# Second layer: reload of the split rows paced by units, the batch two ahead prepared four units sooner, the root ahead of the gathers, and a later store of the row numbers

## The chip, the cores and the metric

One core of one Trainium2 chip runs the whole kernel in one launch. The metric is the device time in microseconds (us), as the median of several runs. Engines are named as the profile names them: PE is TensorE's matmul, PEld its weight load, DVE is VectorE, ACT is ScalarE, POOL is GpSimd, SP is SyncE. SPq marks DMAs that SP's queue issues.

## The reference

Two layers over `x` of 16 batches x 512 rows x 128 columns. The first adds a linear attention (with rotary embedding) and a mixture of experts; the second adds a chunked softmax attention and a gated MLP with a one-row shift. Cut to what matters:

```python
x = L0_attn_x                                   # (16, 512, 128)
xn = layernorm(x)
probs = softmax(xn @ router_w.T)                # 8 experts
topk_p, topk_i = top_k(probs, 2)                # two experts for each row, weights normed to 1
x = x + linear_attention(xn) @ Wo.T + shared_mlp(xn) + sum_e(combine[:, e] * mlp_e(xn))

xn = layernorm(x)
q, k, v = split(xn @ W_qkv.T)                   # 16 heads of 8
for ci in range(n_chunks):                      # chunks of 64 rows, keys up to the chunk's end
    probs = softmax(q_c @ k_c.T / sqrt(8))
    stim = probs.sum(-1)                        # through two steps of a small recurrence
    gate = sigmoid(fhn_dynamics(stim, a, b, dt).mean(-1))
    probs = probs * (0.5 + 0.5 * gate); probs = probs / (probs.sum(-1) + 1e-8)
    out_c = probs @ v_c
x = x + out @ W_out.T + sigmoid(xr @ W_r.T) * (square(relu(xk @ W_k.T)) @ W_v.T)
```

## The kernel before

Each engine runs its own program, written out by hand; semaphores tie them together. Three stages follow one another.

**Stage one** is the first layer's attention and router, batch by batch. It scatters each row's normed copy into a table in HBM, `xs_d`, sorted by expert.

**Stage two** is the experts: 72 tiles of 256 rows (`tile` on every engine). For a tile SP reads the tile's first row and expert out of a table and issues three loads, the rows (`load_rows`, L454) and two weights (`load_weights`, L461 and L462), up to three tiles ahead. PE turns the rows (L1877), multiplies by the first weights (L1889) and by the second (L1898, for the tile before); ACT takes the relu, DVE squares it and copies the result out (L1435, L1441). In tiles 0 to 15 DVE also plans (`planning`): which tiles belong to which expert, and at last, in tile 14, which row of the experts' output belongs to each row of the batches. That last step (L1303) raises `rows_ready`. SP stores these numbers to HBM (`idx_d`, L516) in its step for tile 15, ahead of tile 15's weights and tile 16's rows; they are first loaded back after tile 32.

**Stage three** is the second layer, 17 turns (`body2`, `over_layer2`) for 16 batches. A turn b of PE has 40 units (s, u): four sheets of four heads, ten units each. In each unit PE computes one or two blocks of scores of batch b+1, of which only the row maximum is wanted (`max_scores`, L1944, 44 in a turn; DVE reduces each by `row_max`, L1471, counted as m = 1 to 44), then a block of the shifted scores of batch b (`shifted_scores`, L1967), whose exponential ACT takes (`exp_scores`, L907), and between them products with V (`pv`, L1766). The two banks for the maxima let PE run one block ahead of DVE's reads: the block m + 2 waits for DVE's read of block m.

Round this core lie the steps for other batches, placed by hand at a unit or at an m:

- for b+2: on DVE the two expert outputs are added (`combine`, L1452, m = 2 to 5), the norm's sums taken (`ln_stats_of`, `ln_means`, m = 6 to 8), on POOL the root (`ln_root`, seven small operations, L589 to L601), on DVE the norm (`ln`, m = 14 and 15), on PE the turn (`turn_xn`, (1, 6)) and q and k (`q_rows`, (1, 8) and (1, 9)). Three bf16 parts of q and k are split off by ACT and PE (`hi2`, `mid2`, `lo2`, `take_part`, from (2, 0) to (3, 0)), stored to HBM by SP (`store_parts2`, L497), and loaded back in another layout (`load_half`, L485: two halves of eight DMAs). The first half is wanted by the first `max_scores` of the batch, the second half by its 23rd.
- for b+3: on POOL eight gathers (`gather`, L651), one for 128 rows each, read the experts' output into `hT`.
- for b-1: on POOL, DVE and ACT the recurrence `fhn_*`. It begins with `reweigh_den` on DVE (L1505, m = 16), `fhn_stimulus` on POOL (L665, L667), and `reweigh_scale` on DVE (L1510, m = 18), which waits for L667 by the semaphore `fhn_floor`. At a turn's end DVE writes `output` (L1531), and POOL stores it (L721).

POOL's order in a turn is: the gathers for b+3, the root for b+2, the recurrence for b-1, the store of b-1.

```python
            def reweigh_scale(b):

                dve.wait_ge(fhn_floor, b.at(1, 1 - L2))
                nc.vector.reciprocal(fhn[6][:, :, :], fhn[1][:, :, :]).then_inc(fhn_scale, 1)
```

Of the kernel before, what the change touches and what calls it, by code (L numbers as in the profile page):

```python
# [18 lines left out]
J = T // 128  # L19
# [87 lines left out]
def build(nc, io, out):  # L107
    ctx = ExitStack()
    with ctx:
# [261 lines left out]
        def _(sp):  # L371
# [116 lines left out]

            def store_parts2(n):
                copied = value(sp, n.own(16 * QK_LOADS, -16 * QK_LOADS * HALVES))  # L490
                split_ = [value(sp, n.at(2, c + 1 - 2 * L2)) for c in range(2)]
                for c in range(2):
                    sp.wait_ge(lo_part, split_[c])
                    for h in range(2):
                        if not n.less(L2 + 2):
                            sp.wait_ge(half_loaded[n.p][h], copied)
                    sp.dma_start(parts_d[n.p, c].rearrange("a p t -> p a t"), parts[c][:, :, :]).then_inc(parts_stored[c], 16)  # L497
# [10 lines left out]
            def tile(t):  # L508
# [5 lines left out]
                if k == STRAIGHT * TB - 1:  # L514
                    sp.wait_ge(rows_ready, 1)
                    sp.dma_start(idx_d.rearrange("b p k -> p b k"), idx_all[:, :].rearrange("p (b k) -> p b k", b=B)).then_inc(rows_stored, 16)  # L516
# [13 lines left out]
                if k == LOOPED * TB:  # L530
                    sp.wait_ge(rows_stored, 16)
                    for p in range(2):
                        sp.wait_ge(xa_stored[p], 16 * HALVES)
                    for n in (FIRST, SECOND):
                        load_route(n)
                        load_xa(n)
# [21 lines left out]
            def body2(b):  # L558
                if within(b):
                    shift_rows(b, 1)  # L560
                if within(b + 4):
                    load_route(b + 4)
                    load_xa(b + 4)
                if within(b + 2):
                    store_parts2(b + 2)
                if within(b + 1):
                    shift_rows(b + 1, 0)
                if within(b + 2):
                    load_half(b + 2, 0)
                    load_half(b + 2, 1)  # L570
# [7 lines left out]
        def _(pool):  # L578
# [168 lines left out]
            def body2(b):  # L747
                if within(b + 3):
                    gather(b + 3)
                if within(b + 2):  # L750
                    ln_root(b + 2)
# [11 lines left out]
        def _(act):  # L763
# [198 lines left out]
            def body2(b):  # L962
                core, front, after, before_ = within(b), within(b + 2), within(b + 1), within(b + -1)
                for s in range(SHEETS):
                    for u in range(UNITS):
# [9 lines left out]
                        if at == (1, 4) and after:  # L975
# [3 lines left out]
                        if at == (1, 7) and front:  # L979
                            evac_xnT(b + 2)  # L980
                        if at == (2, 1) and before_:
                            tanh_gate(b + -1)
                        if at in ((2, 0), (2, 2)) and front:
                            hi2(b + 2, u // 2)
                        if at in ((2, 4), (2, 6)) and front:
                            mid2(b + 2, u // 2 - 2)
                        if at in ((2, 8), (3, 0)) and front:
                            lo2(b + 2, s - 2)
# [15 lines left out]
        def _(dve):  # L1004
# [572 lines left out]
            def body2(b):  # L1577
# [3 lines left out]
                def between(m):  # L1581
# [10 lines left out]
                    if m in (6, 7) and front:  # L1592
                        ln_stats_of(b + 2, range(2 * (m - 6), 2 * (m - 6) + 2), False)
                    if m == 8 and front:
# [6 lines left out]
                    if m in (14, 15) and front:  # L1601
                        ln(b + 2, False, range(2 * (m - 14), 2 * (m - 14) + 2))
# [34 lines left out]
        def _(pe):  # L1637
# [416 lines left out]
            def body2(b):  # L2054
# [12 lines left out]
                for s in range(SHEETS):  # L2067
                    for u in range(UNITS):
# [18 lines left out]
                        if where == (1, 2) and after:  # L2087
                            v_rows(b + 1)
                        if where == (1, 6) and front:
                            turn_xn(b + 2, False)  # L2090
                        if where in ((1, 8), (1, 9)) and front:
                            q_rows(b + 2, u - 8)
                        if where in ((2, 2), (2, 4)) and front:
                            take_part(b + 2, u // 2 - 1, 0)
                        if where in ((2, 6), (2, 8)) and front:
                            take_part(b + 2, u // 2 - 3, 1)
# [80 lines left out]
```

## Time and profile before

| | |
|---|---|
| median of 3 runs | 1700.74 us (1698.26 to 1703.08) |
| the profiled execution's own time | 1698.97 us |
| its span, first to last instruction | 1696.8 us, mean granted TensorE clock 0.946 |
| busy share of the span | PE 87%, DVE 70%, PEld 55%, ACT 49%, POOL 31% |
| stage one / two / three | about 0 to 570 / 570 to 884 / 884 to 1697 us |

The page lists what is busy where, not what a stage is worth. The longest stage is the third, so the turn is the unit to look at: DVE's L1531 ends each one, and from one L1531 to the next is one turn. The views used below are the windows (busy time of each engine, granted clock and DMA share in a stretch) and the timelines of single engines.

### The profile page before, as it was taken

How to read it: one execution, taken by the hardware profiler on the slowest of the kernel's cores; microseconds unless marked ns; L12 is line 12 of the kernel's file. 1: busy time of each engine (PE TensorE's matmuls, PEld its weight loads, DVE VectorE, ACT ScalarE, POOL GpSimd, SP SyncE). 2: the span in 40 equal slices, each digit the busy share in tenths (PEclk: the TensorE clock that was granted, in tenths of full speed). 3: DMA queues.
4: the chain of work that ended last, by engine and by line, in shares of the span. 5: the costliest groups of instructions: out<-in, count | busy, mean ns of one | idle time of the engine just before them, and what ended most of it. 6: DMA issues, size and time to landing. Idle time of an engine off the chain costs nothing.

```text
span 1696.8 us, 35053 instructions
## 1 busy us (share of the span) xinstructions
PE 1473.1 (87%) x12952; PEld 934.1 (55%) x12952; DVE 1185.6 (70%) x2666; ACT 823.2 (49%) x1565; POOL 531.9 (31%) x967
## 2 busy tenths in 40 slices
PE   4899998999888798999987988898888898889994
PEld 2566666666666587998873443343444343444431
DVE  4888778788777494455765777777677776778751
ACT  2344344334432333344325656666556665557772
POOL 2422332332331011162314234433434423432223
PEclk7999999999998998999998999999999999999996
DMA  3111111111110656777861345433344433344400
GB/s 109 40 38 45 46 39 45 46 39 45 39 33 26 163 163 200 220 238 215 251 156 51 64 101 101 94 76 71 66 97 101 91 71 73 68 94 83 82 9 12
DMA packets 119082, 152.84 MB, mean 90 GB/s; under 512 B 31348, under 2 KB 83700, under 8 KB 114292
## 3 DMA queue, kind: packets, MB, share of 16 engines
q1 hardware_dynamic: 105992, 120.25, 29.2%
q0 software_dynamic: 12928, 30.43, 6.2%
q8 instruction: 101, 1.65, 0.4%
q14 instruction: 61, 0.50, 0.1%
HBM read 109.01 MB, written 41.09 MB: 88 GB/s over the span
## 4 chain that ended last, share of the span: by engine, by line
PE 55%; DVE 27%; issue 6%; another core or an unknown queue 5%; ACT 2%; SPq 2%; POOL 1%; DMA 1%; DVEq 0%; POOLq 0%; ACTq 0%
PE bank L1766 8%; PE bank L1944 8%; DVE nmax L1471 7%; PE bank L1898 7%; PE bank L1889 7%; PE bank L1967 6%; DVE P L1166 5%; PE bank L1723 3%; PE bank L1666 2%; PE bank L1751 2%; PE bank L1907 2%; PE bank L1783 1%; PE bank L2014 1%; PE bank L1922 1%
## 5 line engine op out<-in xcount | busy, mean ns | idle before, releaser
L1471 DVE TENSOR_REDUCE nmax<-bank 128x1 f32<-128x512 f32 (+3 forms) x704 | 433.9, 636 | 189.0 <-PE bank L1944 144.6
L907 ACT ACTIVATE P<-bank 128x512 f32<-128x512 f32 x640 | 373.8, 597 | 298.8 <-PE bank L1967 230.2
L1944 PE MATMUL bank<-KT,QT 76*128 76x512 bf16 (+3 forms) x1024 | 260.5, 314 | 76.4 <-DVE nmax L1471 48.2
L1967 PE MATMUL bank<-QT,KT 78*128 78x512 bf16 (+3 forms) x1024 | 256.5, 313 | 22.2 <-ACT P L907 13.7
L1944 PEld LDWEIGHTS bank<-KT,QT 76*128 76x128 bf16 x1024 | 88.7, 99 | 265.4 <-DVE nmax L1471 149.2
L609 POOL DMA_INDIRECT xs_d<-xn,idx x128 | 126.1, 985 | 324.0 <-DVE idx L1146 284.6
L1166 DVE TENSOR_TENSOR P<-bank,early_w 128x512 f32<-128x512 f32 x256 | 160.1, 684 | 71.6 <-remote 56.0
L1766 PE MATMUL bank<-P,V 128*32 128x512 f32 (+3 forms) x2048 | 203.4, 471 | 0.0
L871 ACT ACTIVATE hr<-bank 128x512 f32<-128x512 f32 x144 | 86.0, 597 | 192.2 <-PE bank L1889 175.1
L1967 PEld LDWEIGHTS bank<-QT,KT 78*128 78x128 bf16 x1024 | 100.1, 100 | 101.7 <-ACT P L907 39.1
L1435 DVE TENSOR_TENSOR hT<-hr 128x512 f32<-128x512 f32 x144 | 98.2, 691 | 79.1 <-ACT hr L871 77.8
L1889 PE MATMUL bank<-P 128*128 128x256 f32 x576 | 141.0, 389 | 5.0 <-issue 5.0
L1898 PEld LDWEIGHTS bank<-P,hT 128*128 128x128 f32 x1152 | 140.3, 193 | 7.2 <-issue 3.0
L1898 PE MATMUL bank<-P,hT 128*128 128x128 f32 x1152 | 141.3, 276 | 0.6 <-DVE P L1441 0.6
L639 POOL DMA_DIRECT2D ys_d<-P x72 | 52.4, 727 | 252.9 <-DVE P L1441 246.7
L1889 PEld LDWEIGHTS bank<-P 128*128 128x128 f32 x576 | 107.3, 195 | 18.9 <-issue 6.4
L651 POOL DMA_INDIRECT hT<-ys_d,idx x104 | 99.5, 957 | 41.9 <-issue 33.9
L1723 PEld LDWEIGHTS bank<-P,QT 32*128 32x128 f32 x2048 | 70.1, 193 | 59.9 <-issue 59.7
L1723 PE MATMUL bank<-P,QT 32*128 32x128 f32 x2048 | 83.6, 291 | 20.0 <-DVE P L1166 15.9
L1751 PE MATMUL bank<-P,V 128*32 128x128 f32 x2048 | 86.6, 282 | 13.7 <-issue 13.5
L808 ACT COPY oT<-bank 128x512 f32<-128x512 f32 x64 | 37.4, 584 | 97.4 <-PE bank L1751 53.3
L777 ACT ACTIVATE t<-t 128x512 f32<-128x512 f32 x32 | 20.2, 631 | 124.9 <-DVE t L1044 124.9
(233 smaller groups left out, 2263.1 us busy)
## 6 DMA issues: line engine op xcount, KB each, us to landing
P<-in_fc SPq DMA_DIRECT2D x72, 256.0 KB
P<-in_proj SPq DMA_DIRECT2D x72, 256.0 KB
QT<-parts_d SPq DMA_DIRECT2D x96, 192.0 KB
parts_d<-parts SPq DMA_DIRECT2D x32, 384.0 KB, 2.5
P<-xs_d SPq DMA_DIRECT2D x72, 128.0 KB
ys_d<-P POOLq DMA_DIRECT2D x72, 128.0 KB
KT<-parts_d SPq DMA_DIRECT2D x64, 128.0 KB
KT<-parts_d SPq DMA_DIRECT2D x32, 192.0 KB
```

The costliest lines, as they stand in the source:

```text
L609: nc.gpsimd.indirect_dma_start(xs_d[:, :], bass.IndirectOffsetOnAxis(ap=idx[n.p][:, k:k + 1], axis=0), xn[n.p][:, k % J, :], None).then_in ...
L651: nc.gpsimd.indirect_dma_start(gathered_rows(n)[:, k, :], None, rows, bass.IndirectOffsetOnAxis(ap=idx[n.p][:, k:k + 1], axis=0)).then_inc ...
L907: nc.scalar.activation(P[s % 2][:, u, :], bank[k % 2][:, :], ACT.Exp, scale=float(DH) ** -0.5).then_inc(s_sb, 1)
L1166: nc.vector.tensor_tensor(P[s % 2][:, g, :].rearrange("p (j c) -> p j c", c=128), bank[g][:, :].rearrange("p (j c) -> p j c", c=128), tri[ ...
L1471: nc.vector.tensor_reduce(nmax[:, s // TWO, h:h + TWO * nh - 1:TWO, j], max_bank(n, k)[:, 0:nh * w].rearrange("p (h w) -> p h w", h=nh), A ...
L1723: ins = pe.matmul(bank[g][:, tile], kS[b.p][quad, s, tile], qf[b.p][quad, tile], start=True, stop=True)
L1751: ins = pe.matmul(OT[32 * g:32 * g + 32, tile], values(b, j, s, g), P[s % 2][:, g, tile], start=False, stop=(s % TWO == 1 and j == J - 1), ...
L1766: ins = pe.matmul(OT[32 * g:32 * g + 32, 128 * kb:T], values(b, kb, s, g), P[s % 2][:, u, c:c + n], start=(s % TWO == 0 and k == 0), stop= ...
L1889: ins = pe.matmul(w[:, i * GT:(i + 1) * GT], wfc[t.p][:, c * 128:(c + 1) * 128], xgT[t.p % 2], start=True, stop=True)
L1898: ins = pe.matmul(bank[6][:, c * 128:(c + 1) * 128], hT[:, t.p % 2, k, c * 128:(c + 1) * 128], wpj[t.p][:, k, :], start=(k == 0), stop=(k ...
L1944: ins = pe.matmul(max_bank(n, k)[:, i * w:(i + 1) * w], QT[n.p][0:MROWS, h, j * 128:(j + 1) * 128], KT[n.p][0:MROWS, h, 0:w], start=True, ...
L1967: ins = pe.matmul(bank[k % 2][:, c:c + n], KT[b.p][0:SROWS, h, 128 * kb:128 * kb + 128], QT[b.p][0:SROWS, h, 128 * kb:T], start=True, stop ...
```

## The change

It has three parts.

1. **Row numbers.** The wait for `rows_ready` and the store of `idx_d` move from SP's step for tile 15 to its step for tile 32; the loads that read them move from tile 32 to tile 33.
2. **Reload.** SP's eight loads of a half are issued one by one, each after a wait for a unit of PE's (`load_half_at`). The first half of batch b+2 is issued between units 27 and 37 of turn b, the second half of batch b+1 between units 1 and 16 of turn b. Before, both halves were issued in a row at the end of a turn. The two shift rows and the loads for b+4 are now issued between them.
3. **Preparation of b+2.** `ln_stats_of` for all four blocks of rows at m = 6, `ln_means` at m = 7, `ln` at m = 11 and 12 (was 14 and 15); `turn_xn` at (1, 2) (was (1, 6)), `q_rows` at (1, 4) and (1, 5) (was (1, 8), (1, 9)), the splitting four units sooner; `v_rows` and `evac_v2` one and two units sooner. On POOL the root for b+2 comes ahead of the gathers for b+3.

```diff
+            def load_half_at(n, h, b, pieces):
+
+                for k, u in pieces:
+                    sp.wait_ge(s_ps, b.at(PASS, u + 1 - PASS * L2))
+                    load_half(n, h, LOADS[k:k + 1])
...
-                if k == STRAIGHT * TB - 1:
-                    sp.wait_ge(rows_ready, 1)
-                    sp.dma_start(idx_d.rearrange("b p k -> p b k"), idx_all[:, :].rearrange("p (b k) -> p b k", b=B)).then_inc(rows_stored, 16)
...
                 if k == LOOPED * TB:
+                    sp.wait_ge(rows_ready, 1)
+                    sp.dma_start(idx_d.rearrange("b p k -> p b k"), idx_all[:, :].rearrange("p (b k) -> p b k", b=B)).then_inc(rows_stored, 16)
+                if k == LOOPED * TB + 1:
                     sp.wait_ge(rows_stored, 16)
...
             def body2(b):
+                second_half = within(b + 1) and not b.less(L2 + 1)
+                if second_half:
+                    load_half_at(b + 1, 1, b, [(0, 1), (1, 3), (2, 5), (3, 7)])
                 if within(b):
                     shift_rows(b, 1)
+                if second_half:
+                    load_half_at(b + 1, 1, b, [(4, 10), (5, 12), (6, 14), (7, 16)])
                 if within(b + 4):
                     load_route(b + 4)
                     load_xa(b + 4)
                 if within(b + 2):
                     store_parts2(b + 2)
+                if within(b + 2):
+                    load_half_at(b + 2, 0, b, [(0, 27), (1, 28), (2, 29)])
                 if within(b + 1):
                     shift_rows(b + 1, 0)
                 if within(b + 2):
-                    load_half(b + 2, 0)
-                    load_half(b + 2, 1)
+                    load_half_at(b + 2, 0, b, [(3, 31), (4, 32), (5, 34), (6, 35), (7, 37)])
...
             def body2(b):
+                if within(b + 2):
+                    ln_root(b + 2)
                 if within(b + 3):
                     gather(b + 3)
-                if within(b + 2):
-                    ln_root(b + 2)
...
-                    if m in (6, 7) and front:
-                        ln_stats_of(b + 2, range(2 * (m - 6), 2 * (m - 6) + 2), False)
-                    if m == 8 and front:
+                    if m == 6 and front:
+                        ln_stats_of(b + 2, range(J), False)
+                    if m == 7 and front:
                         ln_means(b + 2)
...
-                    if m in (14, 15) and front:
-                        ln(b + 2, False, range(2 * (m - 14), 2 * (m - 14) + 2))
+                    if m in (11, 12) and front:
+                        ln(b + 2, False, range(2 * (m - 11), 2 * (m - 11) + 2))
...
-                        if where == (1, 2) and after:
+                        if where == (1, 1) and after:
                             v_rows(b + 1)
-                        if where == (1, 6) and front:
+                        if where == (1, 2) and front:
                             turn_xn(b + 2, False)
-                        if where in ((1, 8), (1, 9)) and front:
-                            q_rows(b + 2, u - 8)
+                        if where in ((1, 4), (1, 5)) and front:
+                            q_rows(b + 2, u - 4)
+                        if where in ((1, 8), (2, 0)) and front:
+                            take_part(b + 2, s - 1, 0)
                         if where in ((2, 2), (2, 4)) and front:
-                            take_part(b + 2, u // 2 - 1, 0)
-                        if where in ((2, 6), (2, 8)) and front:
-                            take_part(b + 2, u // 2 - 3, 1)
+                            take_part(b + 2, u // 2 - 1, 1)
...
```

POOL, a turn of the steady part of stage three, before: the store of a finished batch (`out`), the gathers (`hT<-ys_d`), the root (`std`, `rstd`), the first steps of the recurrence (`fhn`).

```order
L721 DMA out<-early_w 128x4x128 [waits out_ready,rows_stored]
L651 DMA hT<-ys_d,idx 128x128 [waits x1_ready,route_loaded0,rows_stored]
L651 DMA hT<-ys_d,idx 128x128 x7
L589 TENSOR_TENSOR std<-mv,lnc 128x4 [waits ln_mean]
L591 TENSOR_TENSOR rstd<-std,lnc 128x4 [waits ln_step]
L593 TENSOR_TENSOR std<-std,rstd 128x4 [waits ln_step]
L595 TENSOR_TENSOR std<-std,rstd 128x4 [waits ln_step]
L597 TENSOR_TENSOR std<-std,lnc 128x4 [waits ln_step]
L599 TENSOR_TENSOR std<-std,lnc 128x4 [waits ln_step]
L601 TENSOR_TENSOR rstd<-rstd,std 128x4 [waits ln_step]
L665 TENSOR_TENSOR fhn<-yb,rden 128x64 [waits fhn_den]
L667 TENSOR_SCALAR fhn<-fhn 128x64 [waits fhn_stim]
```

The same place of the changed kernel (its line numbers are 12 higher here):

```order
L733 DMA out<-early_w 128x4x128 [waits out_ready,rows_stored]
L601 TENSOR_TENSOR std<-mv,lnc 128x4 [waits ln_mean]
L603 TENSOR_TENSOR rstd<-std,lnc 128x4 [waits ln_step]
L605 TENSOR_TENSOR std<-std,rstd 128x4 [waits ln_step]
L607 TENSOR_TENSOR std<-std,rstd 128x4 [waits ln_step]
L609 TENSOR_TENSOR std<-std,lnc 128x4 [waits ln_step]
L611 TENSOR_TENSOR std<-std,lnc 128x4 [waits ln_step]
L613 TENSOR_TENSOR rstd<-rstd,std 128x4 [waits ln_step]
L663 DMA hT<-ys_d,idx 128x128 [waits x1_ready,route_loaded0,rows_stored]
L663 DMA hT<-ys_d,idx 128x128 x7
L677 TENSOR_TENSOR fhn<-yb,rden 128x64 [waits fhn_den]
L679 TENSOR_SCALAR fhn<-fhn 128x64 [waits fhn_stim]
```

The root and the gathers have changed places: the gathers now stand behind a wait for `ln_mean`, and directly ahead of the recurrence's first step.

SP, the same part of a turn, before: the second half of a batch's reload, the shift rows, the loads for b+4, the store of the parts.

```order
L485 DMA QT<-parts_d 24x4096 [waits parts_stored0,s_ps]
L485 DMA QT<-parts_d 24x4096 x2
L485 DMA KT<-parts_d 24x4096 [waits parts_stored1]
L485 DMA KT<-parts_d 16x4096
L485 DMA KT<-parts_d 8x4096 x2
L485 DMA KT<-parts_d 16x4096
L506 DMA QT<-shift 1x32x128 [waits shift_hi,s_ps]
L506 DMA QT<-shift 1x32x128 [waits shift_lo]
L468 DMA wts<-wts_d 128x8 [waits x1_ready]
L469 DMA idx<-idx_d 128x8
L474 DMA xt<-xa_d 128x512 [waits res_ready]
L497 DMA parts_d<-parts 128x3x512 [waits half1_loaded1,half0_loaded1,lo_part] x2
```

The same in the changed kernel (L512 is `shift_rows`, L503 `store_parts2`):

```order
L485 DMA QT<-parts_d 24x4096 [waits parts_stored0,s_ps]
L485 DMA QT<-parts_d 24x4096 [waits s_ps] x2
L485 DMA KT<-parts_d 24x4096 [waits parts_stored1,s_ps]
L512 DMA QT<-shift 1x32x128 [waits shift_hi,s_ps]
L512 DMA QT<-shift 1x32x128 [waits shift_lo]
L485 DMA KT<-parts_d 16x4096 [waits s_ps]
L485 DMA KT<-parts_d 8x4096 [waits s_ps] x2
L485 DMA KT<-parts_d 16x4096 [waits s_ps]
L468 DMA wts<-wts_d 128x8 [waits x1_ready]
L469 DMA idx<-idx_d 128x8
L474 DMA xt<-xa_d 128x512 [waits res_ready]
L503 DMA parts_d<-parts 128x3x512 [waits half1_loaded1,half0_loaded1,lo_part] x2
```

Every load of the half has a wait of its own for `s_ps`, PE's count of shifted scores, and the shift rows stand in the middle of them.

## Rows read from the trace of the kernel before

**Rows 1.** Page, busy us of each engine; windows of the three stages
```profile
PE 1473.1 (87%) x12952; PEld 934.1 (55%) x12952; DVE 1185.6 (70%) x2666; ACT 823.2 (49%) x1565; POOL 531.9 (31%) x967
...
core 0: us, PE busy (x) PEld busy (x) DVE busy (x) ACT busy (x) POOL busy (x), PEclk, DMA share, GB/s
0.00:570.00 570.00, 485.83 (x6034) 346.49 (x6034) 425.56 (x1126) 217.49 (x393) 167.74 (x255) 0.96 0.16 47
570.00:884.00 314.00, 290.82 (x1948) 265.89 (x1947) 195.59 (x378) 112.44 (x230) 84.61 (x110) 0.97 0.70 209
884.00:1697.00 813.00, 696.40 (x4973) 321.73 (x4972) 564.49 (x1163) 493.24 (x942) 279.58 (x602) 0.92 0.37 74
```

**Rows 2.** Windows of turns 5, 13 and 2 to 12, same columns
```profile
1138.22:1189.22 51.00, 44.47 (x318) 20.79 (x317) 37.33 (x79) 31.38 (x60) 19.17 (x40) 0.93 0.41 84
1547.47:1591.51 44.04, 41.46 (x318) 19.55 (x317) 37.10 (x78) 31.41 (x60) 11.83 (x32) 1.00 0.41 82
...
986.81:1547.47 560.66, 489.16 (x3478) 227.43 (x3477) 410.60 (x859) 344.71 (x660) 210.61 (x440) 0.93 0.41 84
```

**Rows 3.** Timeline of PE, turn 5: start, length, [idle before <-releaser]
```profile
1149.99 0.34 PE L1944 MATMUL bank<-KT,QT 76*128 76x384 bf16 x1 [1.51 <-issue]
...
1153.03 0.50 PE L1944 MATMUL bank<-KT,QT 76*128 76x384 bf16 x1 [2.49 <-DVE nmax L1471]
```

**Rows 4.** Timeline of POOL, turn 5
```profile
1140.69 1.04 POOL L651 DMA_INDIRECT hT<-ys_d,idx  x1 [0.30 <-issue]
...
1150.52 0.21 POOL L589 TENSOR_TENSOR std<-mv,lnc 128x4 f32<-128x4 f32 x1
...
1153.05 0.20 POOL L601 TENSOR_TENSOR rstd<-rstd,std 128x4 f32<-128x4 f32 x1
1163.77 0.35 POOL L665 TENSOR_TENSOR fhn<-yb,rden 128x64 f32<-128x64 f32 x1 [10.52 <-DVE rden L1505]
1164.20 0.40 POOL L667 TENSOR_SCALAR fhn<-fhn 128x64 f32<-128x64 f32 x1
```

**Rows 5.** Timeline of POOL, turn 0: the second burst of gathers begins
```profile
904.05 1.00 POOL L651 DMA_INDIRECT hT<-ys_d,idx  x1 [0.54 <-issue]
```

**Rows 6.** Timeline of PE, turn 0, in that burst
```profile
910.45 0.39 PE L1944 MATMUL bank<-KT,QT 76*128 76x512 bf16 x1 [0.80 <-issue]
...
916.16 0.34 PE L1944 MATMUL bank<-KT,QT 76*128 76x384 bf16 x1 [2.00 <-DVE nmax L1471]
```

**Rows 7.** Windows of turn 0, with the columns of rows 1
```profile
911.00:916.50 5.50, 2.93 (x31) 1.32 (x29) 2.38 (x4) 2.25 (x5) 2.20 (x3) 1.00 0.15 39
...
916.00:921.00 5.00, 4.84 (x14) 2.08 (x15) 2.01 (x5) 2.59 (x6) 0.00 (x0) 0.66 0.00 0
```

**Rows 8.** Timeline of SP's queue at tiles 14 and 15
```profile
623.74 0.38 SPq L462 DMA_DIRECT2D P<-in_proj  x1
637.27 0.38 SPq L516 DMA_DIRECT2D idx_d<-idx_all  x1
```

**Rows 9.** Timeline of DVE: the last step of the plan
```profile
636.96 0.29 DVE L1303 TENSOR_TENSOR idx_all<-P,moved 128x128 int32<-128x128 f32 x1
```

**Rows 10.** Timeline of PE, tiles 14 to 17
```profile
630.05 1.89 PE L1889 MATMUL bank<-P 128*128 128x256 f32 x8
...
640.91 0.69 PE L1877 MATMUL bank<-ident,P 128*128 128x128 f32 x2 [7.00 <-DMA P<-xs_d]
643.21 3.75 PE L1889 MATMUL bank<-P 128*128 128x256 f32 x8 [1.61 <-issue]
...
649.26 1.89 PE L1889 MATMUL bank<-P 128*128 128x256 f32 x8
...
652.99 1.89 PE L1889 MATMUL bank<-P 128*128 128x256 f32 x8
```

**Rows 11.** Timeline of DVE, turn 13
```profile
1547.47 0.69 DVE L1531 TENSOR_TENSOR early_w<-xr,bank 128x512 f32<-128x512 f32 x1 [0.56 <-PE bank L1994]
...
1557.04 0.37 DVE L1021 BATCH_NORM_AGGREGATE mv<-stats 128x2 f32<-128x6 f32 x4
...
1567.03 0.54 DVE L1510 RECIPROCAL fhn<-fhn 128x64 f32<-128x64 f32 x1
```

**Rows 12.** Timeline of PE, turn 13
```profile
1566.58 0.39 PE L1944 MATMUL bank<-KT,QT 76*128 76x512 bf16 x1 [0.53 <-DVE nmax L1471]
...
1568.52 0.34 PE L1944 MATMUL bank<-KT,QT 76*128 76x384 bf16 x1
...
1568.92 1.02 PE L1907 MATMUL bank<-xnT,wqkv 128*128 128x512 f32 x2
1569.78 0.33 PE L1944 MATMUL bank<-KT,QT 76*128 76x384 bf16 x1
...
1580.71 0.39 PE L1967 MATMUL bank<-QT,KT 78*128 78x512 bf16 x1 [0.57 <-ACT P L907]
```

More of the change, by code:

```diff
@@ L974, in body2 @@
                             evac_oT(b + -1, 1)
-                        if at == (1, 4) and after:
+                        if at == (1, 2) and after:
                             evac_v2(b + 1)
@@ L978, in body2 @@
                             evac_oT(b, 0)
-                        if at == (1, 7) and front:
+                        if at == (1, 3) and front:
                             evac_xnT(b + 2)
@@ L982, in body2 @@
                             tanh_gate(b + -1)
+                        if at in ((1, 6), (1, 8)) and front:
+                            hi2(b + 2, u // 2 - 3)
                         if at in ((2, 0), (2, 2)) and front:
-                            hi2(b + 2, u // 2)
+                            mid2(b + 2, u // 2)
                         if at in ((2, 4), (2, 6)) and front:
-                            mid2(b + 2, u // 2 - 2)
-                        if at in ((2, 8), (3, 0)) and front:
-                            lo2(b + 2, s - 2)
+                            lo2(b + 2, u // 2 - 2)
                         if at == (2, 8) and after:
```

## The prediction, made blind

> **What bounds the kernel.** I read the page first: PE is busy 87% of the span [rows 1], and next to it comes DVE with 70%. Then the windows of the three stages: the third is the longest, 813 us, and has the lowest granted clock, 0.92 against 0.96 and 0.97 [rows 1]. So I cut stage three into turns, from one DVE L1531 to the next, and asked the windows for two of them [rows 2]. Turn 5 takes 51.00 us, turn 13 takes 44.04. Both run 318 matmuls and the same DMA share, 0.41. They differ in one thing: POOL runs 40 operations in turn 5 and 32 in turn 13, because the last gathers belong to turn 12. The 6.96 us split cleanly. PE is busy 3.01 us longer (44.47 against 41.46) at a mean clock of 0.93 against 1.00, and idle 3.95 us longer (6.53 against 2.58). The idle time has a place: two gaps of 1.51 and 2.49 us, at 1149.99 and 1153.03 [rows 3], in which ACT and DVE stand still too. They fall at the end of the eight gathers, which POOL issues from 1140.69 to 1150.5 [rows 4]: the second gap ends 12.3 us after the first gather began. Turns 2 to 12 together take 560.66 us [rows 2], 50.97 each, so all eleven are of this kind.
>
> What makes the gap is the question on which the forecast hangs. In turn 5 the gathers meet the reload's DMAs, all issued at once. But turn 0 holds a burst of gathers with nearly nothing beside it: it begins at 904.05 [rows 5], PE stands 0.80 and 2.00 us (and 0.42 between them) until 916.16, 12.1 us after the burst began [rows 6], and the DMA share there is 0.15 [rows 7]. It is the gathers that bring the gap, with a reload or without. And 2.00 us of idle time is enough to bring the lower clock: 0.66 in the next five us [rows 7], a mix of the 2.4 and the 1.2 GHz level.
>
> In stage two I looked for PE's longest idle time: 7.00 us at 640.91 and 1.61 at 643.21 [rows 10]. SP's queue shows why: after tile 14's weights at 623.74 nothing until 637.27 [rows 8], when DVE's last planning step ends, 636.96 + 0.29 [rows 9]. Tile 15's weights and tile 16's rows stand behind that wait.
>
> **Row numbers.** The rhythm of tiles is 3.73 us, 649.26 to 652.99 [rows 10]. Tile 14's first product starts at 630.05, so tile 16's would start at 637.5 without the wait; it starts at 649.26. I add 0.2, as DVE squares tile 15 only behind its planning step, and 0.2 for the fuller queue: **-11.4 us**, the slow clock behind the gap included. At tile 32 `rows_ready` is some 50 us old, SP runs up to three tiles ahead of PE, and one store costs 0.38 us of issue [rows 8]; the next tile's own waits hide its landing. Bounds: -8.6 (the two gaps alone) to -11.8.
>
> **Reload.** Nothing is added but waits and no byte is saved. The second half's last DMA goes out after unit 16 and is wanted at unit 24; the first half's after unit 37, wanted at unit 4 of the next turn, seven units on. A unit is 44.04 / 40 = 1.1 us, so each has about 8 us to land; even three of them queued find room. The shift rows wait behind three loads and are wanted some 10 us later. I cost it at nothing; the bounds are 0 and +1 a turn if a landing takes over 8 us, which no row shows for these loads. Against this part speaks the Trainium skill, "DMA: Bandwidth & Descriptors", Rules for kernel authors: issue early, wait late. By it pacing can only lose; the rows above leave 8 us, so I leave the sum at nothing.
>
> **Preparation sooner.** The same instructions in other places. On PE, work moved to units (1, 4) and (1, 5) fills idle time that DVE causes, 0.53 us at 1566.58 and as much less before it; the splitting leaves ACT's crowded units, where PE waited 0.57 us at 1580.71 [rows 12]. Bounds 0 and -1.45 (those with 0.35 at (1, 5)); I take -0.9. On DVE the two pairs of `ln` fall on m = 11 and 12, where it is busy already; the root must be there. In turn 13 the sums are done 9.94 us into the turn (1557.41 - 1547.47) [rows 11]; one m sooner makes 9.5. The root takes 2.74 us (1150.52 to 1153.25) [rows 4], so it ends at 12.2, and DVE wants it at 12.7, just in time.
>
> **Root ahead of the gathers.** This is where a new wait comes. The eight gathers take 9.8 us (1140.69 to 1150.52) [rows 4]. They now start behind the root, at 12.5, and end at 22.3 into the turn. Only then do L665 and L667 run (0.35 + 0.40 and their gaps, 0.85 us [rows 4]): 23.2. Who waits is DVE's L1510, which stood at 19.56 in turn 13 (1567.03) [rows 11]. DVE stops there for 3.7 us. Behind it is the reading of maximum 19, and PE's block 21 waits for that read. Block 21 stands at 1568.52 [rows 12], 21.05 into the turn; with `q_rows` moved ahead of it (two times 0.86, 1568.92 to 1569.78) and 0.88 of idle time filled it would come at 21.9. With the wait it comes at 23.3 + 0.54 + 0.6 = 24.4: 2.5 us lost. The burst's own gap falls on the same place: in turn 5 it ended 11.7 us (DVE) after the first gather, here 24.2 instead of 23.3, which makes the block 25.4 and the loss 3.5 us. The gap and the wait overlap; the one covers the other. The loss is over 2.00 us, so the clock falls as before, 3.0 us a turn.
>
> **Sum.** A turn: 44.04 - 0.9 + 3.5 + 3.0 = 49.7, against 50.97: -1.3, times eleven **-14**. Turn 13: **-0.9**. Turn 0 had two bursts, since POOL ran ahead, and turn 1 none; now each has one: turn 0 loses 3.2 of gap and about 1.4 of clock (half of 3.0), turn 1 gains 3.5 + 3.0 - 0.9: **+1**. Together -11.4 - 14 - 0.9 + 1 = -25.3. Against the profiled execution's 1698.97 that is 1673.7; the median of the runs is 1.8 above it. I say **1674**.
>
> **Rivals.**
>
> *The reload was the cause, and pacing cures the gap.* For it: in turn 5 the gap ends as the DMA traffic of the turn ends. Against it: turn 0 [rows 5 to 7]. A turn is then 43.1 plus only the wait of 2.5, and 0 to 3.0 of clock: 45.6 to 48.6. That is -26 to -59 over the eleven, -8 over turns 0 and 1, -0.9 and -11.4: 1620 to 1653. The Trainium skill, "DMA: Bandwidth & Descriptors", Queues, rings and completion order, has each DMA engine go round the queues a packet at a time, so that a gather shares with a backlog; by that rule this rival would hold. The trace of turn 0 disagrees, with its DMA share of 0.15.
>
> *Stage three stays as it is*, what is won at block 21 is lost elsewhere: 51.0 a turn, and stage two alone gives 1698.97 - 11.4 = 1687.6. For it: DVE is full between m = 6 and 13 and POOL's root has 0.5 us to spare.
>
> *The wait behind the gathers comes on top of the gap.* If the gap's end only then lets L665 start, or the gap falls earlier, a turn is 43.1 + 3.95 + 3.7 + 3.0 = 53.8: +31 over eleven turns, +6 for turns 0 and 1, -0.9 and -11.4: 1724, slower than before. It decides from the point at which a turn takes over 52.0, where stage two's gain is spent. For it: L1510 is in DVE's one queue, ahead of all that PE waits for. Against it: L665 needs nothing but POOL's own queue and a semaphore raised 4 us earlier.
>
> *The change does not do what it says*: the order listing shows all three parts in place; no chance.
>
> **How the numbers follow.** Forecast 0.45, cured gap 0.22, stage three unchanged 0.18, wait on top 0.15, of which a third, partly overlapped, lands near no change. About 0.3%, 5 us, is what a measurement of this kernel can tell from nothing, so faster means below 1695.6. The first three lie there: 0.85. Same 0.06, slower 0.09. The range takes in the forecast with its bounds (turns of 48.4 to 51.2), stage three unchanged, and the near part of the cured gap: 1640 to 1692. It leaves out 1724 and the best case.
>
> **What would show it.** In the changed profile: no idle time over 1 us on PE at tile 15, SP's L535 store near 700; that step is right or wrong by itself. On POOL the burst from 12.5 to 22.3 into a turn. Before DVE's reciprocal of the scale (L1522) a wait for POOL of about 4 us; if it is absent, my step on the root is wrong. PE idle 3 to 4 us near 24 into the turn and none at 11 to 15; a clock of 0.93 in the turn's window. If the gap is gone and the clock is 1.00, the reload was the cause. If PE waits for `KT<-parts_d` or `QT<-parts_d` at unit 4 or 24, pacing is too tight.

## The result, and the profile after

The changed kernel takes **1655.87 us** (median of four runs, 1649.84 to 1691.54; the run of 1691.54 fell in a slower state, with a granted clock of 0.928, and is left out of the ratio). The kernel before, timed beside it, takes 1699.5. The ratio is 0.9734, with a 95% interval of 0.9692 to 0.9775: faster by 2.7%; the medians lie 44 us apart. The forecast was 1674 with a range of 1640 to 1692.

The profiled execution spans 1653.4 us against 1696.8. The windows of the three stages of the changed kernel, with the columns of [rows 1]:

```profile
0.00:575.50 575.50, 487.61 (x6036) 348.77 (x6037) 425.40 (x1126) 217.90 (x394) 168.19 (x255) 0.96 0.16 48
575.50:869.10 293.60, 285.72 (x1937) 262.76 (x1936) 192.39 (x373) 112.11 (x229) 83.53 (x109) 0.99 0.75 219
869.10:1653.40 784.30, 696.14 (x4983) 316.23 (x4981) 567.40 (x1168) 491.62 (x942) 281.64 (x603) 0.94 0.30 78
```

The stages are cut here at PE's first product of the first tile and its last product of the last. Cut in the same way, the kernel before has 573.6, 307.2 and 816.0 us. So stage one is 1.9 us longer (nothing in it was changed), stage two 13.6 shorter, stage three 31.7 shorter.

**Stage two.** The timeline of PE of the changed kernel, tiles 14 to 16, and of SP's queue at tile 32:

```profile
631.90 1.89 PE L1901 MATMUL bank<-P 128*128 128x256 f32 x8
...
635.60 0.38 PE L1889 MATMUL bank<-ident,P 128*128 128x128 f32 x2
635.82 1.89 PE L1901 MATMUL bank<-P 128*128 128x256 f32 x8
...
639.87 1.89 PE L1901 MATMUL bank<-P 128*128 128x256 f32 x8
```
```profile
693.10 0.42 SPq L535 DMA_DIRECT2D idx_d<-idx_all  x1
```

The idle times of 7.00 and 1.61 us [rows 10] are gone. Tile 16 starts 7.97 us after tile 14; before, it took 19.21. The store at tile 32 costs 0.42 us of SP's queue and PE waits for nothing behind it.

**Stage three.** The windows of the changed kernel: turns 2 to 12 together, then turn 7, turn 5 and turn 13:

```profile
976.63:1505.03 528.40, 481.87 (x3478) 220.56 (x3477) 410.24 (x858) 343.53 (x660) 212.20 (x440) 0.96 0.34 89
1219.19:1265.59 46.40, 42.37 (x318) 19.65 (x317) 37.27 (x78) 31.02 (x60) 19.29 (x40) 1.00 0.36 92
1121.20:1170.42 49.22, 45.45 (x318) 20.51 (x317) 37.39 (x79) 31.30 (x60) 19.31 (x40) 0.93 0.33 87
1505.03:1548.25 43.22, 41.79 (x318) 19.76 (x317) 37.11 (x79) 31.19 (x60) 11.49 (x32) 1.00 0.31 81
```

Against [rows 2] the eleven turns are 32.3 us shorter, 48.04 each in place of 50.97. They are no longer alike: five take 46.35 to 46.40 at the full clock, the other six 47.9 to 51.1 with a lower one. Turn 13 has lost 0.82 us.

In turn 7 the timeline of POOL answers to [rows 4]:

```profile
1231.15 0.20 POOL L613 TENSOR_TENSOR rstd<-rstd,std 128x4 f32<-128x4 f32 x1
1231.89 1.07 POOL L663 DMA_INDIRECT hT<-ys_d,idx  x1 [0.54 <-issue]
...
1240.86 0.95 POOL L663 DMA_INDIRECT hT<-ys_d,idx  x1 [0.30 <-issue]
1241.83 0.35 POOL L677 TENSOR_TENSOR fhn<-yb,rden 128x64 f32<-128x64 f32 x1
1242.28 0.40 POOL L679 TENSOR_SCALAR fhn<-fhn 128x64 f32<-128x64 f32 x1
```

The timeline of DVE, and under it that of PE, at the same place:

```profile
1237.65 0.69 DVE L1483 TENSOR_REDUCE nmax<-bank 128x1 f32<-128x512 f32 x1 [1.50 <-PE bank L1956]
...
1242.70 0.55 DVE L1522 RECIPROCAL fhn<-fhn 128x64 f32<-128x64 f32 x1 [1.47 <-issue]
```
```profile
1241.29 0.34 PE L1956 MATMUL bank<-KT,QT 76*128 76x384 bf16 x1 [0.43 <-DVE nmax L1483]
1242.57 0.39 PE L1979 MATMUL bank<-QT,KT 78*128 78x384 bf16 x2 [0.95 <-issue]
...
1244.20 0.34 PE L1956 MATMUL bank<-KT,QT 76*128 76x384 bf16 x1 [0.67 <-DVE nmax L1483]
```

The burst runs from 12.70 to 22.6 us into the turn, L679 ends at 23.5, and DVE's L1522 starts at that moment. (The profile names no releaser for the 1.47 us ahead of it; in eight of the other ten turns it names L679, with 1.5 to 5.2 us.) The gaps of 1.5 and 2.5 us that stood at 11 to 15 us are gone from there. In this turn PE's idle time is spread over pieces of less than 1 us between 16 and 25 us. Over the eleven turns its longest piece is 0.85 to 1.81 us where the clock stays full, and 0.93 to 4.61 us where it falls.

### The profile page after: what moved, and what is told of

The parts are those of the page before. It is cut to its first block, busy times and chain, and to the rows that moved or that the text cites. A ratio compares the mean times of both kernels' runs of the same rounds, so it can differ in the third digit from the quotient of the medians.

```text
span 1653.4 us, 35249 instructions
## 1 busy us (share of the span) xinstructions
PE 1469.5 (89%) x12952; PEld 927.8 (56%) x12952; DVE 1185.2 (72%) x2666; ACT 821.6 (50%) x1565; POOL 533.4 (32%) x967
## 4 chain that ended last, share of the span: by engine, by line
PE 50%; DVE 28%; issue 7%; ACT 5%; POOL 4%; another core or an unknown queue 4%; SPq 1%; DMA 1%; DVEq 0%; POOLq 0%; ACTq 0%
DVE nmax L1483 8%; PE bank L1910 7%; PE bank L1901 7%; PE bank L1778 6%; PE bank L1956 6%; DVE P L1178 5%; PE bank L1979 5%; ACT P L919 3%; PE bank L1735 3%; PE bank L1678 3%; PE bank L1763 3%; POOL hT L663 2%; PE bank L2026 1%; PE bank L1889 1%
## 5 line engine op out<-in xcount | busy, mean ns | idle before, releaser
L1178 DVE TENSOR_TENSOR P<-bank,early_w 128x512 f32<-128x512 f32 x256 | 160.0, 684 | 71.7 <-remote 56.2
```

The source lines that it names most:

```text
L1178: nc.vector.tensor_tensor(P[s % 2][:, g, :].rearrange("p (j c) -> p j c", c=128), bank[g][:, :].rearrange("p (j c) -> p j c", c=128), tri[ ...
```

## The experiments

The theory going in (A): a burst of gathers stalls the engines wherever it stands, and the change lets that stall overlap DVE's wait behind the burst. The rival (B): the reload's traffic made the gap, and pacing cured it. There are twelve runs of nine kernels, in four groups; in each group the kernel before was timed beside them.

The groups fell on **two levels**. In the first and the fourth group the kernel before took 1697.9 and 1696.8 us, like the result above; in the second and the third it took 1561.1 and 1565.7, with the same instructions. I call them level one and level two. Times in us are compared within a level only; turn lengths also across, where the text says so. What sets the level the runs don't tell. The chip alone seems not to: by the numbers on record the four groups ran on chips 1, 6, 3 and 6, so that chip 6 was first at level two and later at level one. Whether it is the core on the chip, a neighbour or something else is open. Some of the expectations below speak of "a chip like the first" or "the second"; read level one and level two. The experiments at level two and the section on the hardware show what differs.

### Row numbers alone (level one)

```diff
 # the kernel before, with
-                if k == STRAIGHT * TB - 1:
-                    sp.wait_ge(rows_ready, 1)
-                    sp.dma_start(idx_d ...).then_inc(rows_stored, 16)
                 if k == LOOPED * TB:
+                    sp.wait_ge(rows_ready, 1)
+                    sp.dma_start(idx_d ...).then_inc(rows_stored, 16)
+                if k == LOOPED * TB + 1:
```

> The kernel before with only the later store of the row numbers. My theory: PE's idle time of 7.0 and 1.6 us at tile 15 goes, nothing else changes: -11.4 us (-8.6 to -11.8), a ratio to before of 0.9933; turns of stage three stay at 51 us. Rival: the wait only moves to a later tile (SP behind the store at tile 32, or the weights' buffers): 0 to -4 us.

Measured 1684.36 against 1697.9, ratio 0.9932 (0.9913 to 0.995). Its windows of turns 2 to 12:

```profile
968.95:1530.27 561.32, 490.58 (x3478) 228.28 (x3477) 410.54 (x859) 344.71 (x660) 211.38 (x440) 0.93 0.41 84
```

51.03 us a turn: this part works in stage two and nowhere else. A second run of the kernel, in the fourth group (the text below was on record for it), gave 0.9935 (0.9909 to 0.996) and 50.97 us a turn.

> The kernel before with only the later store of the row numbers, again; stage three is that of the kernel before. On a chip on which the kernel before takes some 1562 us: theory A (the burst brings no gap there) says turns of 44 to 45 us at full clock with POOL's eight gathers at 2.5 to 12.5 us of the turn as before, and -11 us, a ratio of 0.993. Rival: the gap is there and only its clock cost is not: 48 us a turn. On a chip with 1698 us: as the first time, 51.0 us a turn and 0.993.

It was meant to show stage three of the kernel before at level two, and came out at level one. So there is no profile of that stage, with its gathers in place, at level two.

### The reload at once again (level one)

```diff
 # the changed kernel, with
-                    load_half_at(b + 1, 1, b, ...)
-                    load_half_at(b + 2, 0, b, ...)
 ...
                 if within(b + 2):
+                    load_half(b + 2, 0)
+                    load_half(b + 2, 1)
```

> The changed kernel with both halves of the reload issued in a row at the turn's end again, as before; the new order on POOL, the sooner preparation and the row numbers' move stay. Theory A (the burst of gathers makes the gap, the reload does not; what won in stage three is that the gap now overlaps DVE's wait behind the burst): the same turns as the changed kernel, 46.4 where the clock stays full and 49 to 51 where it falls, and the time within 8 us of the changed kernel's 1656. Theory B (pacing cured the gap): turns of 50 to 51 again, time 1680 to 1690.

Measured 1649.90 us, ratio 0.9727 (0.971 to 0.9745). The windows of turns 2 to 12:

```profile
970.23:1497.93 527.70, 481.90 (x3478) 220.31 (x3477) 409.82 (x858) 343.94 (x660) 212.14 (x440) 0.96 0.43 89
```

527.70 us against 528.40 with pacing. The DMA engines are busier (0.43 against 0.34) and nothing else moves. **Pacing does nothing for the time** at this level; theory B, which said 50 to 51 us a turn and 1680 to 1690, falls.

### The gathers ahead of the root again (level one)

```diff
 # the changed kernel, POOL
+                if within(b + 3):
+                    gather(b + 3)
                 if within(b + 2):
                     ln_root(b + 2)
-                if within(b + 3):
-                    gather(b + 3)
```

> The changed kernel with the gathers ahead of the root on POOL, as before; pacing, sooner preparation and the row numbers' move stay. Theory A: the burst starts at 2.5 us of the turn again, the gap of 1.5 and 2.5 us stands at 11 to 15 us, DVE's norm at m = 11 waits for the root until 15 us on top, the clock falls in each turn: 51 to 52 us a turn, time 1687 to 1700. Theory B: no gap, only the wait for the root: 46 us a turn, time 1650.

Measured 1673.03, ratio 0.9864 (0.9846 to 0.9881). Windows of turns 2 to 12, and DVE in a turn that begins at 1219.90:

```profile
970.78:1519.42 548.64, 491.12 (x3478) 229.85 (x3477) 409.92 (x858) 341.52 (x660) 211.41 (x440) 0.93 0.33 86
```
```profile
1232.32 0.69 DVE L1483 TENSOR_REDUCE nmax<-bank 128x1 f32<-128x512 f32 x1 [3.08 <-remote]
```

The gap is back at 12.4 us into the turn, and the clock falls in each turn. A turn takes 49.88 us. I had expected 51 to 52 and a time of 1687 to 1700: the wait for the root did not come on top, since DVE is held up by the gap at that same place. So the order on POOL is worth 1.84 us a turn of the 2.93 won, and the sooner preparation 1.09. That division holds for preparation with the gathers ahead of the root; the two parts don't simply add, as the next two runs show.

### Only the order on POOL (level two)

```diff
 # the kernel before, POOL
+                if within(b + 2):
+                    ln_root(b + 2)
                 if within(b + 3):
                     gather(b + 3)
-                if within(b + 2):
-                    ln_root(b + 2)
```

> The kernel before with only the root moved ahead of the gathers on POOL. The sums are done 9.9 us into the turn, so the burst runs from some 13 to 23 us and DVE's reciprocal of the scale waits until 24 us. Theory A (the gap and the wait overlap): 46.5 to 48 us a turn where the clock stays full, up to 51 where it falls; time 1655 to 1680, that is nearly all of the changed kernel's gain in stage three comes from this one swap. Rival (the sooner preparation makes the gain): 50 to 51 us a turn, time 1690 to 1700.

Measured 1635.35 against 1561.12: ratio **1.0469** (1.0433 to 1.0504), slower. Windows of turns 2 to 12, then DVE and PE in a turn that begins at 1174.65:

```profile
918.89:1482.01 563.12, 482.12 (x3478) 223.87 (x3477) 409.07 (x858) 345.64 (x660) 215.38 (x440) 0.93 0.41 83
```
```profile
1199.49 0.55 DVE L1510 RECIPROCAL fhn<-fhn 128x64 f32<-128x64 f32 x1 [4.80 <-POOL fhn L667]
```
```profile
1200.65 0.50 PE L1944 MATMUL bank<-KT,QT 76*128 76x384 bf16 x1 [4.48 <-DVE nmax L1471]
```

Here the wait that the prediction feared stands alone and in full: DVE stops for 4.80 us behind L667, PE for 4.48, and the clock falls in each of the eleven turns. A turn takes 51.19 us, where turn 13, without gathers, takes 44.04. Neither of my cases can be judged by its time: both took for granted that the kernel before takes 51 us a turn, as at level one, and at this level it does not. So what the swap alone does to the kernel before at level one was not seen.

### The changed kernel at level two

The changed kernel itself, nothing edited.

> The changed kernel again, timed on the same chip as the kernel before. The two chips so far differ: the kernel before took 1698 us on the first and 1561 on the second, where turns without the gap took 44.0 us. On a chip like the first, where a burst of gathers brings the gap: 0.974 again, turns of 46.4 at full clock and 49 to 51 where it falls. On a chip like the second, theory A (what the change leaves in each turn is DVE's wait behind the gathers, and there it has no gap to hide in): turns of 46 to 50 us against 44 to 45 before, stage two 11 us shorter, ratio 1.00 to 1.03. Theory B (the order is harmless with the sooner preparation): ratio 0.985.

Measured 1590.26 against 1565.72: ratio **1.0165** (1.0136 to 1.0194). At this level the change makes the kernel *slower*. Windows of turns 2 to 12, then DVE and PE in the turn that begins at 1147.32:

```profile
908.30:1437.30 529.00, 480.65 (x3467) 221.99 (x3477) 407.75 (x858) 343.73 (x660) 212.07 (x440) 0.95 0.35 89
```
```profile
1170.82 0.55 DVE L1522 RECIPROCAL fhn<-fhn 128x64 f32<-128x64 f32 x1 [3.33 <-POOL fhn L679]
```
```profile
1171.97 0.34 PE L1956 MATMUL bank<-KT,QT 76*128 76x384 bf16 x1 [2.71 <-DVE nmax L1483]
```

The turns are as long as at level one (48.09 us against 48.04), but made differently. DVE arrives on time and waits for POOL for 3.33 us in one piece; at level one it arrives late, by nearly the same sum. That is the overlap of theory A, seen from both sides, and its times for this level, 46 to 50 us a turn and a ratio of 1.00 to 1.03, came true. The row numbers still win: stage two, cut as above, is 294.1 us here, against 305.8 in the kernel with direct loads and the old store, shown next. Against the run before, the sooner preparation wins too: 48.09 us a turn in place of 51.19. The burst starts 12.7 us into the turn and not 14.1, and DVE's wait behind it is 1.5 us shorter. With the root first it is therefore worth 3.1 us a turn, not the 1.09 found above.

### Direct loads in place of the gathers (level two, twice)

```diff
 # the kernel before, POOL
-                    nc.gpsimd.indirect_dma_start(gathered_rows(n)[:, k, :], None, rows, ...)
+                    pool.dma_start(gathered_rows(n)[:, k, :], ys_d[128 * k:128 * k + 128, :])
```

> The kernel before, whose eight gathers of a batch are replaced by eight direct loads of the same size from the same table and the same queue (what is left out: the choice of rows by index, so the second layer works on other rows). Theory A (the gap belongs to the indirect DMAs that POOL works out): it goes although the reload still arrives at once; turns of 44 to 45 us at full clock, time 1615 to 1635. Theory B (it is traffic on the DMA engines or POOL's queue, the reload's above all): the gap stays at 11 to 15 us of the turn, 50 to 51 us a turn, time 1690 to 1700.

> The kernel before with direct loads in place of the gathers (rows not chosen by index), on the same chip as the run beside it. On a chip like the first: theory A (the gap belongs to the indirect DMAs): turns of 44.0 us, ratio 0.945 to 0.955; theory B (traffic or POOL's queue): 50 to 51 us a turn, ratio 0.99 to 1.00. On a chip like the second: 0.992 again.

Measured 1550.86 against 1561.12 (ratio 0.992, 0.9888 to 0.9951) and 1551.06 against 1565.72 (0.991, 0.9886 to 0.9934). The windows of turns 2 to 12 of the second, and POOL's eight loads:

```profile
913.42:1398.03 484.61, 455.57 (x3467) 214.95 (x3477) 407.91 (x858) 345.63 (x660) 176.72 (x440) 1.00 0.49 97
```
```profile
1135.74 4.25 POOL L651 DMA_DIRECT2D hT<-ys_d  x8
```

Turns of 44.06 us, as turn 13. But the kernel before is only 10 to 15 us slower at this level, about 1 us for each of the 13 bursts; with turns of 51 it would be some 90 us slower (13 by 7). So, from the times alone, **at level two the burst brings almost no gap**, and the question that this kernel was made for (is it the indirect DMAs, or any burst from POOL?) was not put, since neither run fell on level one. It stays open.

### Five gathers, then three (level one)

```diff
 # the changed kernel, POOL
                 if within(b + 3):
-                    gather(b + 3)
+                    gather(b + 3, range(5))
                 if within(b + -1):
                     fhn_stimulus(b + -1)
+                    pool.wait_ge(fhn_scale, ...)
+                    nc.gpsimd.tensor_tensor(f2, f0, f6, ALU.mult).then_inc(fhn_step, 1)
+                if within(b + 3):
+                    gather(b + 3, range(5, 2 * J))
+                if within(b + -1):
                     fhn_two_steps(b + -1)
```

(The recurrence's first product is taken out of `fhn_two_steps`.)

> The changed kernel with five gathers behind the root, then the recurrence's first three steps on POOL, then the other three gathers, in the 3.7 us in which POOL waits for ACT's gate. Theory A with the gap tied to the length of a burst: DVE's reciprocal of the scale no longer waits (5 gathers end at 19 us of the turn), turns of 43.2 to 44 us at full clock, time 1615 to 1630. Theory A with the gap tied to each gather: the wait goes but 2 to 3 us of short gaps stay, 45 to 46 us a turn, time 1640 to 1650. Rival: the three late gathers only push the recurrence back by 1 us and nothing is won: 1656.

Measured 1619.12, ratio **0.9542** (0.9504 to 0.9579). Windows of turns 2 to 12:

```profile
969.97:1464.28 494.31, 464.45 (x3478) 217.58 (x3477) 406.54 (x858) 342.99 (x660) 213.18 (x440) 0.99 0.35 95
```

44.94 us a turn, 3.1 less than the changed kernel, and the clock falls in only two of the eleven. The time lies in the range of the first case, the turn between it and the second. DVE no longer waits for POOL, and the stall of the burst's second half is smaller; as the split takes both away at once, this run can't say how much of the 3.1 us belongs to which. In a turn of 44.30, the one that begins at 1194.50, what is left over turn 13's 43.22 is mostly a stall of DVE of 1.5 us that ends 5.7 us after the first gather began.

### Five and three, with the reload at once (level two)

The edits of "the reload at once again" and "five gathers, then three" together.

> Five gathers, the recurrence's first steps, three gathers, with both halves of the reload issued at once at the turn's end. Theory A: as with the paced reload, 44.3 us a turn, time within 8 us of 1619. Theory B (traffic makes the gap): turns of 46 us or more, time 1635 or more.

Measured 1533.10 against 1561.12, ratio 0.9809 (0.977 to 0.9848); 43.53 us a turn:

```profile
906.09:1384.93 478.84, 459.93 (x3478) 217.24 (x3477) 407.88 (x859) 343.32 (x660) 212.67 (x440) 1.00 0.46 98
```

With the reload at once there is no gap here. That says little of theory B, since even a burst of eight brings almost none at this level. My time of 1619 was for the other level.

### Three, three and two (both levels)

```diff
 # as five and three, but gather(b + 3, range(3)) and range(3, 6), and
                     fhn_weights(b + -1)
+                if within(b + 3):
+                    gather(b + 3, range(6, 2 * J))
```

> Three gathers behind the root, three in POOL's wait for ACT's gate, two behind the recurrence, where POOL stands idle. The run with five and three has 44.3 us a turn against 43.2 in the turn without gathers, and an idle time of DVE of 1.5 us 5.7 us after the first gather. If that comes with the fourth and fifth gather of a burst: 43.2 to 43.7 us a turn, time 1605 to 1615. If each gather costs its share wherever it stands: 44.3 us, time 1612 to 1623. Rival: the last two land too late for the next turn's addition of the experts' outputs at m = 2 to 5: over 45 us, time over 1625.

> Three, three and two gathers, again. On a chip with 1562 us for the kernel before: 43.3 us a turn and a ratio of 0.980 again. On a chip with 1698 us: theory A with the gap tied to the length of a burst: 43.3 to 44.0 us a turn, faster than five and three (0.954), ratio 0.945 to 0.952. If each gather costs its share wherever it stands: 44.3 to 45 us a turn, ratio 0.953 to 0.960.

Measured at level two 1531.70 against 1561.12, ratio **0.9803** (0.9766 to 0.984), and at level one 1594.93 against 1696.77, ratio **0.940** (0.9372 to 0.9428). Windows of turns 2 to 12, first at level two, then at level one:

```profile
907.31:1383.42 476.11, 459.72 (x3478) 217.50 (x3477) 408.03 (x858) 343.06 (x660) 213.34 (x440) 1.00 0.39 99
```
```profile
970.87:1449.30 478.43, 460.51 (x3478) 217.19 (x3477) 407.39 (x859) 343.90 (x660) 214.12 (x440) 1.00 0.39 98
```

43.28 and 43.49 us a turn: with bursts of three at most, eight gathers cost 0.1 and 0.3 us of a turn, and the clock never falls. At level one the turn lies where it should if the stall comes with the length of a burst (43.2 to 44.0), and not where each gather costs its share; the times, 1594.93 us and a ratio of 0.940, are lower than either case said. The last two, issued behind the recurrence, land in time. POOL at level one, in the turn that begins at 1232.10:

```profile
1247.51 0.95 POOL L663 DMA_INDIRECT hT<-ys_d,idx  x1 [0.30 <-issue]
1251.23 0.35 POOL L677 TENSOR_TENSOR fhn<-early_w,rden 128x64 f32<-128x64 f32 x1 [2.77 <-DVE rden L1522]
...
1253.55 1.03 POOL L663 DMA_INDIRECT hT<-ys_d,idx  x1 [0.41 <-issue]
...
1266.35 1.05 POOL L663 DMA_INDIRECT hT<-ys_d,idx  x1
```

POOL waits for DVE now, and DVE no longer for POOL. At level one this is the fastest version; at level two it is as fast as five and three with the reload at once (1533.10), and wins where the changed kernel loses.

## Why the prediction was right, and where not

**Right in sign, low in size.** Forecast -25, measured -44 (the two profiled executions: -43). The time lies in the range.

**Row numbers: -11.4 forecast, and right.** From tile 14 to tile 16 it is 19.21 - 7.97 = 11.24 us. Stage two as a whole is 13.6 shorter, but the other 2.4 us lie behind tile 16, and are scatter and not gain: from tile 16 to the stage's end the profiles have 229.2 to 233.8 us with the edit and 229.8 to 231.9 without it. The ratios of the two runs with this edit alone, 0.9932 and 0.9935, are -11.5 and -11.0 us.

**Reload: nothing forecast, nothing measured** (527.70 against 528.40 us over eleven turns). The argument from turn 0, a gap with a DMA share of 0.15, pointed the right way.

**Preparation sooner: -0.9 forecast, -0.82 in turn 13**, and -1.09 where the gathers stay ahead of the root. What I left out is that it also lets the burst begin sooner once the root is first: at level two that makes it 3.1 us.

**Turns 0 and 1: +1 forecast.** From the last tile's product to the end of turn 1 the changed kernel takes 107.6 us, before 106.0: +1.6.

**Root ahead of the gathers.** The times into the turn came out as worked out: the root's end 12.2 (12.16), the burst 12.5 to 22.3 (12.70 to 22.6), L679's end 23.2 (23.5). At the full clock a turn is 43.1 + 3.5 = 46.6 by the forecast and 46.38 by the trace. The overlap of gap and wait, on which the forecast hung against the rival of 1724, holds: at level two, where there is almost no gap, DVE waits 3.33 us in one piece, and the one turn at the full clock takes 46.02, hardly less than 46.38. One sign that I gave came out otherwise: at level one DVE's wait before L1522 is mostly 1.5 us and not about 4, because the gap has already held DVE up by some 1.5 us before it gets there.

**The step that failed** is the last of that part: "The loss is over 2.00 us, so the clock falls as before, 3.0 us a turn." It falls in six turns of eleven, and the mean excess over a turn at the full clock is 48.04 - 46.38 = 1.66 us, a few longer stalls included. Over all eleven turns that is 1.34 us a turn less than the 3.0, 15 of the 18 us by which the forecast missed. The price of a fall was right: the six turns take 49.4 on average, 3.0 above 46.38. What was wrong is that every turn would pay it. I took the loss as one piece of idle time of over 2 us, as before. At level one it is split by matmuls in most turns; only two have a piece over 2 us (3.18 and 4.61), and both lose the clock. At level two it is one piece of 2.7 us or more in every turn, and the clock falls in ten of eleven; the one turn that keeps it has the same 2.71 us, so "over 2.00 us" alone doesn't decide it. Why it falls in one turn with small pieces and not in the next stays open.

**What the forecast lacked** is that its largest cost, the gap, is not a property of the kernel. Turn 0 showed that the gathers bring it with or without traffic; it could not show that at another level they hardly bring it. There the change is slower than the kernel before, as the third rival had it, but not for its reason: the wait doesn't come on top of a gap, it comes where there was almost none to save. The forecast was made from a trace at level one and measured at level one; that the time moved the right way is owed to that, and that was luck. The order on POOL is a gain only as a place to hide the gap, and the split does away with both.

## What to carry to other kernels

A burst of indirect DMAs on GpSimd's queue can cost twice: what stands behind it waits (3.33 us at level two), and at level one all engines stall in its second half (1.51 and 2.49 us in turn 5 of the kernel before). Spread such a burst over the queue's own idle times, two or three at once; over the eleven turns at level one, moving the burst whole had won 20 us; splitting it won 34 more as five and three, and 50 more as three, three and two. Before believing that a move is a gain, ask whether it removes a wait or only lays it over another stall: take the stall away and see what is left.

## What the hardware showed that was not expected

**The same kernel at 1562 and at 1697 us.** The work itself is no faster at level two: the changed kernel's turn 13, without gathers, takes 43.22 us at both levels, and its stage two 293.6 and 294.1. What is missing is stalls in stretches where indirect DMAs run. In stage three these are the gaps above. In stage one, whose scatters are indirect too, the page's group of DVE's L1178 in the changed kernel reads, at level one and at level two:

```profile
L1178 DVE TENSOR_TENSOR P<-bank,early_w 128x512 f32<-128x512 f32 x256 | 160.0, 684 | 71.7 <-remote 56.2
```
```profile
L1178 DVE TENSOR_TENSOR P<-bank,early_w 128x512 f32<-128x512 f32 x256 | 158.7, 682 | 37.8 <-PE bank L1735 37.8
```

One instruction takes 684 and 682 ns, but the idle time ahead of the 256 is 71.7 and 37.8 us, and 56.2 of the first has no releaser on this core that the profile can name. Stage one takes 575.5 us at level one and 517.3 at level two, which is most of the difference between the levels for this kernel; another 10.7 us lie in turns 0 and 1. That the stalls are late semaphore updates during indirect DMAs fits these rows; it was not tested by itself.

**The clock does not go by the longest idle time.** In the changed kernel a turn whose longest idle time of PE was 1.81 us kept the full clock; one with 1.82 us, at the same place of the turn, lost it, and so did one whose longest was 0.93 us:

```profile
1001.57 0.34 PE L1956 MATMUL bank<-KT,QT 76*128 76x384 bf16 x1 [1.82 <-DVE nmax L1483]
...
1099.82 0.34 PE L1956 MATMUL bank<-KT,QT 76*128 76x384 bf16 x1 [1.81 <-DVE nmax L1483]
```
```profile
1193.76 0.39 PE L1979 MATMUL bank<-QT,KT 78*128 78x384 bf16 x2 [0.93 <-issue]
```
```profile
1001.00:1006.00 5.00, 4.25 (x21) 1.53 (x21) 3.22 (x6) 4.70 (x10) 1.12 (x4) 0.72 0.33 80
...
1099.00:1104.00 5.00, 4.00 (x26) 1.79 (x27) 3.68 (x7) 4.79 (x11) 1.17 (x4) 1.00 0.29 80
...
1194.00:1201.00 7.00, 6.51 (x31) 2.11 (x29) 4.02 (x7) 5.22 (x11) 1.58 (x5) 0.53 0.22 57
```

The granted clock is 1.00 (2.4 GHz) after the 1.81 us, 0.72, a mix of 2.4 and 1.2 GHz, after the 1.82, and 0.53, nearly all at 1.2 GHz, after the 0.93. The Trainium skill, "TensorE: Matmul & The Clock Gate", Part 1, has the monitor's window run free of the kernel; by that rule equal idle times can cost the clock in one turn and not in the next, which agrees with these rows.
